# Causal small attention: the second half's weighted sums three slots later, with the values and output pieces around them

## What is computed

```python
q = x @ Wq.T + bq;  k = x @ Wk.T + bk;  v = x @ Wv.T + bv      # x: 16 sequences (2 x 8), 256 x 128, normalised
q = apply_rope(q.reshape(b, l, N, H).transpose(0, 2, 1, 3)) * scale     # N, H = 16 heads, 8 features
k = apply_rope(k.reshape(b, l, N, H).transpose(0, 2, 1, 3))
dots = jnp.einsum('bnih,bnjh->bnij', q, k)
dots = jnp.where(i[:, None] < i[None, :], -100000.0, dots)
o = jnp.einsum('bnij,bnjh->bnih', jax.nn.softmax(dots, axis=-1), v)
return o.transpose(0, 2, 1, 3).reshape(b, l, d) @ Wo.T + bo             # added to the stream
```

## Time and profile before

| | us |
|---|---|
| median of 3 runs | 4698.73 (4696.16 to 4699.51) |
| the profiled execution | 4698.96 |
| its span, first to last instruction | 4697.2 |
| PE busy in the span | 3784.2 (81%) |
| DVE busy | 3316.0 (71%) |
| POOL busy | 2399.8 (51%) |
| ACT busy | 2369.2 (50%) |
| stage l1att, in the span | about 2103 to 2457 |
| stage gqa, in the span | about 3649 to 3982 |

### The profile page before, as it was taken

One profiled execution on the slowest core, in us unless ns is written; L12 is line 12 of the kernel. 1 busy time (PEld: TensorE's weight loads), 2 busy tenths in 40 slices (PEclk: granted clock), 3 DMA queues, 4 the chain that ended last, 5 costly groups with the idle time before them and its releaser, 6 DMA issues. The chain is left out here.

```text
span 4697.2 us, 90969 instructions
## 1 busy us (share of the span) xinstructions
PE 3784.2 (81%) x25828; PEld 2709.6 (58%) x25828; DVE 3316.0 (71%) x9072; ACT 2369.2 (50%) x5659; POOL 2399.8 (51%) x3960
## 2 busy tenths in 40 slices
PE   7888799779999879778878977468776788779875
PEld 5666566756666556566655657423322566456565
DVE  7888688456666678656557875569998665478756
ACT  3444466455555556544445554545554454246545
POOL 5666554434333445446653554367776564035543
PEclk9999899889999989888988998789989899989988
DMA  6000233200000033233313322212221331033223
GB/s 253 0 0 0 83 114 110 74 23 1 0 1 0 9 124 126 72 114 110 106 66 125 122 83 64 73 50 64 64 61 52 118 115 66 0 120 121 86 61 91
DMA packets 244140, 343.48 MB, mean 73 GB/s; under 512 B 26672, under 2 KB 186816, under 8 KB 242688
## 3 DMA queue, kind: packets, MB, share of 16 engines
q1 hardware_dynamic: 230528, 310.64, 20.0%
q0 software_dynamic: 13184, 27.81, 1.7%
HBM read 183.42 MB, written 148.64 MB: 71 GB/s over the span
## 5 line engine op out<-in xcount | busy, mean ns | idle before, releaser
L1218 POOL TENSOR_TENSOR wb_prob<-wb_prob,wb_rden 128x128 f32<-128x128 f32 (+1 forms) x512 | 248.2, 506 | 377.9 <-DVE wb_rden L1395 377.5
L793 DVE TENSOR_REDUCE l0att_rowmax<-l0att_S 128x2 f32<-128x512 f32 x512 | 340.3, 686 | 88.4 <-PE l0att_S L1026 81.8
L793 DVE TENSOR_REDUCE l1ffn_rowmax<-l1ffn_S 128x2 f32<-128x512 f32 x512 | 341.4, 685 | 80.8 <-PE l1ffn_S L1026 75.3
L2094 POOL TENSOR_TENSOR ssm_hc<-core_AW_all,ssm_Cs 128x512 f32<-128x512 f32 x256 | 321.1, 1270 | 129.7 <-DVE core_AW_all L2240 96.0
L1260 ACT ACTIVATE wb_prob<-wb_biased,wb_nmax 128x128 f32<-128x128 f32 (+1 forms) x512 | 228.6, 447 | 252.9 <-DVE wb_nmax L1388 250.0
L1691 POOL DMA_INDIRECT results<-e_y,e_back x220 | 211.0, 959 | 270.2 <-DVE e_y L1818 171.3
L2339 PE MATMUL ssm_Y<-ssm_hc,core_ident 128*128 128x512 f32 x512 | 288.1, 673 | 56.0 <-POOL ssm_hc L2094 29.6
L1026 PE MATMUL l1ffn_S<-l1ffn_K,l1ffn_Q 128*128 128x512 f32 x512 | 252.0, 496 | 82.5 <-DVE l1ffn_rowmax L793 47.1
L1026 PE MATMUL l0att_S<-l0att_K,l0att_Q 128*128 128x512 f32 x512 | 256.0, 503 | 72.9 <-DVE l0att_rowmax L793 42.3
L2240 DVE TENSOR_TENSOR_SCAN core_AW_all<-core_AW_all,ssm_U 128x512 f32<-128x512 f32 x256 | 310.3, 1212 | 0.8 <-ACT core_AW_all L2183 0.8
L2183 ACT ACTIVATE core_AW_all<-ssm_dt,ssm_A 128x510 f32<-128x510 f32 x256 | 178.5, 716 | 221.5 <-DVE core_AW_all L2240 219.8
(11 more groups left out here) (509 smaller groups left out, 11502.6 us busy)
## 6 DMA issues: line engine op xcount, KB each, us to landing
bounce<-l0att_parts SPq DMA_DIRECT2D x128, 256.0 KB
bounce<-l1ffn_parts SPq DMA_DIRECT2D x128, 256.0 KB, 2.8
ssm_Cs<-c_rows SPq DMA_DIRECT2D x128, 256.0 KB, 3.0
routed<-core_Y SPq DMA_DIRECT2D x8, 2176.0 KB, 26.0
l0att_Q<-bounce SPq DMA_DIRECT2D x128, 128.0 KB
l0att_K<-bounce SPq DMA_DIRECT2D x128, 128.0 KB
bounce<-l1att_parts SPq DMA_DIRECT2D x64, 256.0 KB
l1ffn_Q<-bounce SPq DMA_DIRECT2D x128, 128.0 KB
```

The costliest lines, as they stand in the source:

```text
L793: dve.tensor_reduce(out=rowmax[:, jp, qt, 2 * pair:2 * pair + 2], in_=S[a % 2][:].rearrange("p (j k) -> p j k", j=2)[:, :, 0:keys(qt)], op ...
L1218: ins = pool.tensor_tensor(out=prob[:, w_ % NP, a:b], in0=prob[:, w_ % NP, a:b], in1=rden[:, w_ % NP, n:n + 1].to_broadcast([P, b - a]), o ...
L2094: pool.tensor_tensor(out=hc[:, u % 4], in0=hs[:, u % 4], in1=Cs[:, n % 4], op=ALU.mult)\
```

## The change

For the causal stages, a table of slots is altered. The second half's weighted sums move from slots 1 and 2 to 4 and 5, ACT's copy of them from slot 3 to 6. "v" moves from slot 4 to 6, "n0" from 5 to 8, "n1" from 6 to 12, "on" from 12 to 14, and "out" from slot 14 to slot 0 two rounds after the sequence's own, which makes one more round at the end. "mt1", "h", "qq", "kk" and "mt0" keep their slots. The scores, turns, selects, parts and the order of SP's DMAs stay as they are.

```diff
         if rope:
-            plan = {3: "mt1", 4: "v", 5: "n0", 6: "n1", 7: "h", 9: "qq", 10: "kk", 11: "mt0", 12: "on", 14: "out"}
+            plan = {0: "out", 3: "mt1", 6: "v", 7: "h", 8: "n0", 9: "qq", 10: "kk", 11: "mt0", 12: "n1", 14: "on"}
...
         ahead = {"h": 3, "qk": 3, "qq": 3, "kk": 3, "v": 2, "mt0": 1, "mt1": 0, "n0": -1, "n1": -1, "on": -1,
-                 "out": -1, "yt": -2, "lg": -2}
-        ROUNDS = range(-3, SEQS + (3 if router else 1))
+                 "out": -2 if causal else -1, "yt": -2, "lg": -2}
+        SECOND_AT = 4 if causal else 1
+        ROUNDS = range(-3, SEQS + (3 if router else 2 if causal else 1))
...
-                for jp, at in ((1, 3), (0, 13)):
+                for jp, at in ((1, SECOND_AT + 2), (0, 13)):
...
-                    for jp, at in ((1, 1), (0, 10)):
+                    for jp, at in ((1, SECOND_AT), (0, 10)):
```

## The result

The changed kernel takes **4724.57 us** (median of 5 runs, 4711.19 to 4729.11), where the kernel before takes 4698.73 (4689.77 to 4703.93) on the same chip: the ratio is 1.0058, 95% interval [1.0038, 1.0078]. It is slower by about 26 us. 4711 was forecast; the sign and the range held, the loss is twice the forecast's +12. The profiled execution has a span of 4722.8 us against 4697.2, so the two traces carry 25.6 us to be found.

What follows compares the result with a forecast made beforehand. Rounds of l1att and gqa were taken as bound by the mask and transfer chains from kk, the transfer remaining after the change. gqa +20, l1att −4 and ends −4 gave +12 on 4698.73: 4711 us, range 4680 to 4731.

Steps and rivals of the forecast that it cites:

- Step 1: Second half's sums at slots 4 and 5: PE comes 2.4 us later, so the mask wait goes; "mt1" may wait 0.3.
- Step 5: Slot 8: kk to slot 8 stays 14.3 us, PE then waits 2.1 (gqa) and 2.0 us (l1att) for K.
- Step 4: SP: next first half's sends issued while the second half's still land; no cost taken, bound 1 us a round.
- The clock: PE's clock falls after the slot 8 wait, in slots 8 to 10: 1.1 us a round in gqa, 1.0 in l1att.
- the likeliest case: Both causal stages: K wait replaces the mask wait and the clock falls after it; 4711 us, chance 0.49.
- Rival A: Same K wait at slot 8 in both stages, but the clock holds: 4684 us, chance 0.18.
- Step 2: "n0" from slot 5 to 8: 0.7 us less between kk and slot 8, 0.5 more between slot 8 and kk.
- The ends of the stages: Rounds 14 and 15, with no store behind: some 2 us really won in each stage, together −4.
- C: Clock falls in half of the rounds or fewer, +0.5 us a round: 4697 us, no change, chance 0.14.
- D: First half's sends, issued early, slow the second half's: 1 us × 26 rounds on top, 4737 us, chance 0.12.
- B: K comes earlier too, PE alone sets rounds of 17.4 us in both stages: 4628 us, chance 0.07.

Runs made afterwards that it cites:

- experiment 6: The changed kernel with v, h, qq, kk one slot earlier (5, 6, 8, 9), mt0 at 10 and n0 at 11: 4675.29 us, ratio 0.9945.
- experiment 4: The changed kernel with one more wait on SP, so the next first half's sends are issued only once the second half's have landed: 4713.68 us, ratio 1.0034.
- kernel 3: The changed kernel with eight unneeded 512-column matmuls ahead of slot 8's score, filling PE's wait for K: 4690.69 us, ratio 0.9986.
- kernel 8: The changed kernel with v at slot 4, h 5, qq 7, kk 8, n0 9, mt0 10: 4628.57 us, ratio 0.9850.

## Why the prediction came out as it did

**Step 1, right.** The mask wait is gone in both stages, and "mt1" waits 0.4 us (0.3 forecast).

**Step 5, right in kind, a little short.** The wait for K took its place: 2.1 us in l1att (2.0 forecast), 2.6 in gqa (2.1). kk to slot 8 takes 14.8 us and not 14.3. The 14.3 came from one round of the earlier trace rows; the mean of the rounds 1 to 12 of the kernel before was 14.5 already (14.75 in the same rounds now), so some 0.2 us is a term read from one quick round, and the rest is step 4. The chain itself was read wrongly in one place: slot 8 does not need the rows of the stores ahead of its sends, as "PE scores slot 8 with those rows" has it. They are of the sequence after, and only SP's order ties the two (experiment 6). For this change the sum comes out the same.

**Step 4, wrong.** Overlapping sends were taken as free, with 1 us as the bound. They cost about 0.2 us a round and, with shorter waits and fewer falls, some 11 us of the time (experiment 4). The argument was that the queue behind is idle anyway; it speaks of the later group and says nothing of the earlier one.

**The clock, right in kind, short in gqa.** This was the likeliest case's largest term. Forecast were 1.0 us a round in l1att and 1.1 in gqa, three to four falls in five rounds; measured 1.0 and about 1.55. l1att had 8 falls in twelve rounds, one of them of double length. gqa had 11, three of double length: 14 single ones, at the forecast's 1.4 us each 1.6 a round. So the price of a fall was right and their number in gqa too small; the waits there are the longer ones. 13 x 0.45 = 6 us. Rival A (the clock holds) would have given 4684, and kernel 3, in which it holds, gives 4691: its arithmetic was sound and its condition false.

**Step 2, half.** n0 between slot 8 and kk costs some 0.35 us of that stretch (0.5 forecast) but only 0.16 to 0.34 of the round.

**The ends of the stages** were credited with 4 us, and gave 3.6: thirteen rounds grew by 27.8 us in gqa (276.87 less 249.11) and shrank by 0.6 in l1att, while the two stages as a whole, from PE's first to its last matmul, grew by 23.5. Another 2 us of the 25.6 lie in stages that weren't touched.

Put together, the trace lost 25.6 us where +12 was forecast, 13.6 more. Kernel 3 tells the round at full clock: 19.77 in gqa and 19.83 in l1att (means of thirteen), 0.17 and 0.33 above the forecast's 19.6 and 19.5: K comes 0.5 later than the 14.3 (steps 4 and 5), and slot 8 to kk is 0.1 to 0.2 shorter than the 5.2. That is 2 + 4 us in thirteen rounds. The clock's part is 21.30 - 19.77 = 1.53 in gqa (1.1) and 20.75 - 19.83 = 0.92 in l1att (1.0), +6 and -1 us. With 0.4 for the ends and 2 from elsewhere this makes the 13.6. The path was as predicted; the mis-sized terms are the falls in gqa and the time from kk to slot 8.

**Rivals.** A is excluded by the trace and by kernel 3. C (falls in half of the rounds or fewer) is excluded: there are falls in 8 of 12 and 11 of 12. D's mechanism is there with a fifth of its price. B (K comes early, and PE alone sets the round) was given 4628 with rounds of 17.4. It didn't come with this change, but kernel 8 made its condition true and reached 4628.57 with 17.1; that the totals agree to a microsecond is chance. What the prediction didn't see is the third chain through the buffer, and DVE's row maxima behind it; neither closed a round of the changed kernel, and both cut what one expects of an earlier kk.

## What to carry to other kernels

When a wait is removed, list every chain that starts at the same instruction and take the next longest as the new bound; if all of them start there, move the start (here kk, 70 us) and not the end (here the sums, -26). Two short waits can be better than one long one of the same sum: here the clock fell far more often after the long one. And before an issue is moved earlier, look at what stands ahead of it in its queue and who frees its buffer: when kk was moved by one slot, SP's order and the falls after the wait that it left took away 41 of the 69 us expected, and once the order was mended, the buffer became the bound.

## What the runs showed of the hardware

- TensorE's granted clock fell to 0.50 for 3.4 us, at times 6.8, near 88 of 109 waits of 2.0 us and more in a loop that is otherwise dense, and near 1 of 76 waits of 1.0 to 1.5 us. Eight needless matmuls in each such wait won 34 us in 26 rounds.
- A second group of four 128 KB sends, issued 2 to 3.4 us before the first has landed, delays the first by about 0.2 us.
